# A windowed attention layer without the one-column identity matmuls ahead of its small-tile matmuls

## The reference

```python
t = x.reshape(B, C, N).transpose(0, 2, 1)          # B 4, C 384, N 4096; x is group-normalised
qkv = t @ qkv_w.T                                  # 8 heads of 48 channels
scores = einsum('bhnqd,bhnkd->bhnqk', q, k) * scale   # inside chunks of 64 tokens
attn = softmax(scores, axis=-1)
out = einsum('bhnqk,bhnkd->bhnqd', attn, v)
out = out @ proj_w.T + proj_b
```

## Time and profile before

| what | value |
|---|---|
| median of 3 runs | 6866.09 us (6865.48 to 6866.52) |
| the profiled execution | 6863.25 us, its span 6861.5 us |
| mean granted TensorE clock | 0.939 of full speed |
| TensorE matmul busy | 5990.6 us (87%) |
| VectorE busy | 6138.1 us (89%) |
| ScalarE busy | 4716.2 us (69%) |
| GpSimd busy | 5351.3 us (78%) |

### The profile page before, as it was taken

The page is one execution under the profiler, slowest core; times in us unless marked ns, Lnnn a source line. Parts: engine busy times, 40 slices in busy tenths (PEclk is TensorE's granted clock), DMA queues, the critical chain, the costliest instruction groups (busy, mean ns, idle before and its releaser), DMA issues. The chain is left out here.

```text
span 6861.5 us, 99209 instructions
## 1 busy us (share of the span) xinstructions
PE 5990.6 (87%) x32906; PEld 3756.6 (55%) x32906; DVE 6138.1 (89%) x7731; ACT 4716.2 (69%) x8759; POOL 5351.3 (78%) x4333
## 2 busy tenths in 40 slices
PE   4888888888888888888888888888888879999998
PEld 2455555555555555555555555555555547777776
DVE  4899999999999999999999999999999956666665
ACT  1777777777777777777777777777777743333332
POOL 0999999999999999999999999999999930101010
PEclk9999999999999999999999999999999989999999
DMA  4322222222222222222222222222222232222222
GB/s 186 114 112 111 112 109 112 102 101 101 100 102 101 101 101 103 104 101 102 100 101 102 100 101 104 104 101 102 101 101 101 108 125 71 78 79 77 81 73 68
DMA packets 177702, 694.99 MB, mean 101 GB/s; under 512 B 28332, under 2 KB 28556, under 8 KB 143140
## 3 DMA queue, kind: packets, MB, share of 16 engines
q1 hardware_dynamic: 177188, 688.65, 27.0%
HBM read 512.57 MB, written 157.09 MB: 98 GB/s over the span
## 5 line engine op out<-in xcount | busy, mean ns | idle before, releaser
L774 POOL TENSOR_TENSOR dbx<-u,bb 128x512 f32<-128x512 f32 x3072 | 3829.4, 1280 | 29.9 <-DVE p_da L673 14.8
L673 DVE TENSOR_TENSOR_SCAN p_da<-p_da,state_v,dbx 128x512 f32<-128x512 f32 x2112 | 2620.8, 1273 | 54.6 <-ACT p_da L548 54.6
L548 ACT ACTIVATE p_da<-dt,neg_a 128x512 f32<-128x512 f32 x3076 | 2076.1, 687 | 83.6 <-DVE h L680 8.2
L898 PEld LDWEIGHTS p_yt<-ident,hc_v 128*128 128x128 f32 x8448 | 1108.8, 151 | 1137.1 <-issue 843.0
L898 PE MATMUL p_yt<-ident,hc_v 128*128 128x128 f32 x8448 | 1381.5, 293 | 162.9 <-DVE hc_v L689 162.4
L689 DVE TENSOR_TENSOR hc_v<-cc,p_da 128x512 f32<-128x512 f32 x2112 | 1391.4, 666 | 0.0
L783 POOL TENSOR_TENSOR hc_g<-h,cc 128x512 f32<-128x512 f32 x960 | 1227.6, 1279 | 108.4 <-DVE h L680 108.3
L680 DVE TENSOR_TENSOR_SCAN h<-p_da,state_g,dbx 128x512 f32<-128x512 f32 x960 | 1218.1, 1269 | 103.8 <-ACT p_da L548 103.5
L839 PE MATMUL p_g<-xs,win 128*128 128x512 f32 x2376 | 1208.6, 603 | 74.7 <-ACT zt L500 36.3
L554 ACT ACTIVATE state_v<-p_da 128x1 f32<-128x1 f32 x2112 | 351.0, 166 | 914.2 <-DVE hc_v L689 901.8
L1321 POOL TENSOR_TENSOR x_low<-axn,x_upper 128x512 fp32r<-128x512 f32 x96 | 127.3, 1355 | 1045.9 <-DVE x_upper L1273 1045.9
(11 more groups left out here) (153 smaller groups left out, 7397.5 us busy)
## 6 DMA issues: line engine op xcount, KB each, us to landing
bb<-bc_spill SPq DMA_DIRECT2D x132, 1024.0 KB, 10.4
cc<-bc_spill SPq DMA_DIRECT2D x132, 1024.0 KB, 10.2
xc_spill<-xc SPq DMA_DIRECT2D x99, 512.0 KB, 2.6
z_spill<-zt SPq DMA_DIRECT2D x99, 512.0 KB, 3.9
xj<-xc_spill SPq DMA_DIRECT2D x193, 256.0 KB, 4.1
zj<-z_spill SPq DMA_DIRECT2D x192, 256.0 KB, 2.7
xs<-in_x SPq DMA_DIRECT2D x34, 768.0 KB, 5.7
xc<-in_x SPq DMA_DIRECT2D x33, 768.0 KB, 11.9
```

The costliest lines, as they stand in the source:

```text
L548: nc.scalar.activation(p_da[n % RD][:], dt[:, d % 2, :], ACT.Exp, scale=neg_a[:, d, n:n + 1])\
L673: nc.vector.tensor_tensor_scan(psum, psum, dbx[:, n % RB, :], state_v[:, d, k:k + 1], ALU.mult, ALU.add).then_inc(s_scan, 1)
L774: nc.gpsimd.tensor_tensor(dbx[:, n % RB, :], u[:, d % 2, :], bb[:, n, :], ALU.mult)\
L898: last = nc.tensor.matmul(p_yt[d % 2][:, b * P:(b + 1) * P], product[:, b * P:(b + 1) * P], ident[:], start=False, stop=n == NS - 1, is_tr ...
```

## The change

The two identity matmuls are taken out. Nothing else is edited.

```diff
@@ scores
                 pe.wait_ge(s_dv, w * 7 - 3 + C_ATT)
-
-                nc.tensor.matmul(p_s[0][:, 0:1], ident[:], ident[:, 0:1], start=True, stop=True)
                 for uu in range(NU):
@@ weigh
                 pe.wait_ge(s_oc, w * 2 + C_ATT)
-
-                nc.tensor.matmul(p_o[0][:, 0:1], ident[:], ident[:, 0:1], start=True, stop=True)
                 for uu in range(NU):
```

## The result

The changed kernel took 6837.1 us, the median of 6 runs (6834.92 to 6840.48). Six runs of the kernel before took 6865.05 to 6869.6 us, 6866.31 in the median. The ratio is 0.9957, with a 95% interval of 0.9945 to 0.997: the change makes the kernel 0.43% faster. The forecast was 6836.6 us.

What follows compares the result with a forecast made beforehand. TensorE was taken to bound the attention layer. Savings of 14.1 (scores), 7.4, 6.8 and 1.2 us (weigh) sum to 29.5, so 6863.25 becomes 6833.75 us; plus 2.84, the median forecast is 6836.6 us, range 6812 to 6860 us.

Steps and rivals of the forecast that it cites:

- one wait: Steady attention groups: TensorE's transposes of step 3, turn(3), wait for VectorE's last softmax product, 0.9 us each, 27.7 us in all.
- All 8 sites are on the path, as the wait hangs on weigh(2): Each group's identity matmuls: bringing weigh(2) forward brings VectorE's copy and product forward equally; the wait stays 0.93 us.
- A site costs 0.11 to 0.12 us: Scores and weigh behind full-width slices: removing the identity saves 0.11 us, or 0.12 us for weigh behind a qk slice.
- The pause before a change of shape: Between full-width and small matmuls on TensorE: 0.09 us beyond the last matmul's pace, with or without the identity.
- the 2.84 us between execution and median: Whole kernel: the median lies 2.84 us above the profiled execution, turning 6833.75 us into 6836.6 us.
- The clock of the end: Last group and last projections: a lower granted clock can give or take some 1.9 and 2.5 us; costed at zero.
- rival 1: Scores and weigh sites: small loads hide under the last full-width matmul; 52.8 us saved, 6813 us; chance 0.10.
- rival 2: Scores and weigh sites: the pause lasts to the long matmul's modelled end; 12.5 us saved, 6854 us; chance 0.10.
- rival 3: Scores and weigh sites: without the identity the first small load is exposed; 22.8 us more, 6889 us; chance 0.11.
- Rival 4: Attention groups: nothing changes, because a wait takes the saving up; 6866 us; chance 0.04.
- The lower bound: Range's fast end, 6812 us: no pause before small matmuls, saving 0.20 us in scores and 0.21 in weigh.
- the sign that the scan layer should end where it did: Scan layer, ahead of attention: in the changed kernel's trace its end should not move.

Runs made afterwards that it cites:

- two of eight: Against the kernel before, the identity matmuls of scores(3) and weigh(2) alone, of a group's eight, are taken out; 6859.12 us, ratio 0.9989.
- the kernel with the normalising first: Against the changed kernel, VectorE normalises a step ahead of copying the previous step's weighed values, instead of behind; 6800.29 us.
- The one-pass kernel: Against the kernel before, each identity matmul is replaced by a single-pass full-width matmul of two columns; 6837.62 us, ratio 0.9958.
- the double one: Against the kernel before, two identity matmuls stand at every site instead of one; 6925.98 us, ratio 1.0086.
- the two half changes: Against the kernel before, the identity is taken out of scores alone (6852.89 us) or of weigh alone (6848.69 us).
- the kernel with both orders: Against the changed kernel, some scores blocks stand directly behind weigh on TensorE, and VectorE normalises ahead of its copy; 6779.55 us.

## Why the prediction was right

- **TensorE bounds the attention layer, with one wait.** Right: removing TensorE work alone shortened the period by 0.87 us, at the same idle time.
- **All 8 sites are on the path, as the wait hangs on weigh(2).** Right. The kernel with two of eight shows that the wait doesn't take up the saving, and the kernel with the normalising first shows by which instruction it hangs there.
- **A site costs 0.11 to 0.12 us, the second load of the identity.** The change confirms the size: 0.27, 0.33 and 0.52 us where 0.27, 0.32 and 0.53 were worked out. The one-pass kernel and the double one confirm that it is the second pass: with one pass the matmul costs nothing, two more passes cost 0.23 us. That it is the load within the pass is pointed to by equal paces and not separated by a run. The sites of scores and of weigh gave alike, 0.46 us for four; the periods of the two half changes fell by 0.40 and 0.50 us since the qk slices also moved.
- **The pause before a change of shape is 0.09 us.** Right, as a size. It was read from a change of columns behind 128-column transposes and holds for tiles of 64 rows behind matmuls of 384 and 512 columns. Whether the trace's time lies in a drain of the array or in something else isn't shown; what is shown is that it doesn't grow with the length of the matmul in front, and that between blocks of equal shape it isn't there. As each modelled end lies about as far behind the pace, "pace plus 0.09 us" and "0.07 us before the modelled end" give the same times here, and no run tells them apart.
- **The sum.** 29.5 us was forecast, 30.2 us less is the attention layer's length in the profiles, and 29.2 us less is the median. The period was forecast as 37.63 us and is 37.66. That the forecast of the median is only 0.5 us off is in part luck. The sites gave 0.91 us a group, the qk slices took 0.07 us of it back and the values 0.03 us less, neither of which was in the sum. And the 2.84 us between execution and median were carried over from the kernel before, while the changed kernel's profiled execution is 0.7 us above its median. The clock of the end, costed at zero, made 0.5 us.
- **The rivals.** Hidden small loads (rival 1) would have given 0.18 us at scores, a full wait for the modelled end (rival 2) 0.34, an exposed load (rival 3) 0.48; it is 0.27. Rival 4 would have left the period at 38.53.
- **What was too coarse.** The lower bound took the small loads to hide completely, although both changes of shape in the trace spoke against it; it made the range 24 us wide on that side for a chance of 0.10. And the 4.8 us by which the two profiled executions differ ahead of the attention layer were not thought of: the sum was made for an execution, and one execution moves by about that much at the start alone. So the sign that the scan layer should end where it did didn't hold in these two: the attention layer began 4.8 us later. The end was priced a little high as well: 4.48 us is with a modelled end, and in the chain the six slow matmuls took 4.28 us against 2.58 at full clock, 1.7 and not 1.9 us.

## What to carry to other kernels

When TensorE bounds a stage, what an instruction costs is the distance of starts around it with and without it, not its busy time: the identity's two passes were 0.4 us busy and 0.11 us long. Ask of a wait which instruction it hangs on before calling a saving absorbed; here the same reading that showed that nothing is absorbed pointed to an order on VectorE that was worth more (1.15 us a group) than the change itself (0.87). Where small-tile matmuls alternate with full-width ones, put the small blocks next to each other: each round trip of shapes cost 0.34 us here. Then look at the first groups too: the kernel with both orders lost some 4 us there to a wait that the steady groups don't have.
